# Scatter windows of 144 destination columns in place of 160 in a four-layer graph network

## Chip, cores and metric

One Trainium2 chip, one of its cores. The metric is the device time of one execution in microseconds (us), lower is better. Before: 2755.7 us, the median of three runs (2754.37 to 2758.44).

## The reference, cut to what matters

6250 nodes with 128 features each, 100000 edges sorted by destination node, four message-passing layers. Layers 0 and 1 (the first two) add relu(x[src] + edge attribute) into the destination node, then an MLP with a batch norm; layers 2 and 3 (the last two) add x[src] alone and apply another MLP.

```python
...
dst = jnp.minimum((6250 * jax.random.uniform(..., (100000,)) ** 2.0).astype(jnp.int32), 49999)
_o = jnp.argsort(dst, stable=True)
src = src[_o]
dst = dst[_o]
...
msg = jax.nn.relu(x[src] + edge_attr)
agg = jax.ops.segment_sum(msg, dst, num_segments=N_NODES)
h = (x + agg) @ W1l + b1l
...
agg = jax.ops.segment_sum(x[src], dst, num_segments=x.shape[0])
h = (1.0 + eps) * x + agg
...
```

## The kernel before, in words

The edges are cut into 196 groups of 512 (`SUPERS`), and four groups make a turn of 2048 edges, 49 turns to a layer (`TURNS`). A turn has two windows (`HALVES`), each of two groups, 1024 edges. Since the edges are sorted, the destinations of one window lie close together; the window begins at the smallest of them and is `WIN` columns wide. How many such windows, laid side by side, are needed for the widest pair of groups is worked out on the chip (`reached_f`, line 1352: the multiples of `WIN` that do not exceed the widest pair's spread are counted into `rounds`), and every scatter loop runs `rounds` times.

One edge stage (layers 0 and 1, `edges`) has five steps for each turn:

- POOL gathers the source rows from the node table in HBM with indirect DMAs, 128 rows of 512 bytes each (line 675), 16 to a turn; in two turns of each layer one group's four are replaced by row loads on SP's queue. Its buffer `xg` holds three turns, and POOL waits on `summed` (line 672) before it uses one again.
- ACT copies the edge attributes into PSUM (line 759), DVE adds the gathered rows to them (`slot_sum`, line 1131), ACT applies the relu to half a turn (line 786).
- DVE builds a one-hot matrix (`set_windows`, line 1077): for each of 16 columns of 128 edges, `WIN` columns of which the one of the edge's destination is 1. So it writes 16 x `WIN` elements to a partition.
- PE multiplies messages by one-hots (`edge_windows`, line 1510): 16 float32 matmuls to a turn, `WIN` columns each, into `psG`. The trace shows two matmul records for each.
- DVE adds the two windows to the accumulator `acc` at columns read from `first_i` (`add_windows`, line 1061, the instruction in line 1030).

Beside that, while the edge stages run, DVE and PE count how often each source meets each destination for the first 34 turns of edges (lines 1096, 1117 and 1494), ACT evicts the counts (line 742), and SP stores them to HBM (line 587). In the final turn of a layer the order on DVE is another one: the one-hot of the final turn is built ahead of its message sums (line 1153), and the windows of the last two turns are added at the end.

Layers 2 and 3 (`counted_edges`) use those counts: PE multiplies features by counts (line 1537, 147 matmuls of 456 columns for a group of 12 units), which stands for the first 34 turns; the last 15 turns are still gathered and scattered as windows. So PE alternates half a group of counts (72 or 75 matmuls) with one turn's windows (`late_windows`, line 1552, again 16 float32 matmuls of `WIN` columns and 32 records). POOL gathers those turns with 16 indirect DMAs each (line 695), 240 to a layer, into two buffers: turn k+2 waits until PE has finished the windows of turn k (`reduced`, line 691), and on the indices that ACT copies when a turn's rows have landed (line 831). DVE builds the one-hots (line 1202) and adds the windows. SP loads the next half group of counts, some 2.8 MB, when PE has finished with the buffer (line 596). In the last layer DVE adds a bias over all nodes in one instruction (line 1228), behind its first one-hots.

The turns of the counted layers are numbered 0 to 14 below, and POOL's gathers in one such layer 1 to 240.

What the change touches: the constant `WIN` (line 33), and by it lines 36, 313, 315, 320 (sizes), 651 (the offsets of the windows), 1061, 1077, 1187, 1202, 1510 and 1552.

```python
first_i[:, q, :] = min(pair_f + round_off, NODES)
...
rows[p, c, w] = (loc_all[p, c] - round_off == iota[w])
...
acc[:, first:first + WIN] += psG[:, q, h * WIN:(h + 1) * WIN]
...
```

Of the kernel before, what the change touches and what calls it, by code (L numbers as in the profile page):

```python
# [29 lines left out]
HALVES = (range(0, 2), range(2, SLOTS))  # L30
WINDOWS = len(HALVES)
PAIRED = SUPERS // 2
WIN = 160
BLOCKS = -(-NODES // P)
PADDED = BLOCKS * P
ACC = PADDED + WIN
GB = 4
# [151 lines left out]

assert TURNS % 2 == 1 and 2 * SLOTS * EPP * WIN <= CELL_RING * CB  # L190
assert SUPERS % SLOTS == 0 and OVERLAP % EPP == 0 and SECOND <= P
# [27 lines left out]
def gnn_kernel(nc, x, src, dst, edge_attr, W1, b1, gamma, beta, W2, b2,  # L219
               w1a, b1a, w1b, b1b, eps1, w2a, b2a, w2b, b2b, eps2, out):  # L220
    with ExitStack() as ctx:
        ctx.enter_context(nc.allow_non_contiguous_dma(reason="columns of biases"))

        def sb(name, shape, dt=F32):
            return ctx.enter_context(nc.sbuf_tensor(name, shape, dt))

        def sem(name):
# [84 lines left out]

        hot = hid[:, 0:2 * SLOTS * EPP * WIN].rearrange("p (q u j w) -> p q u j w", q=2, u=SLOTS, j=EPP)

        late_hot = rows_h[:, :, :].rearrange("p b d -> p (b d)")[:, 0:2 * SLOTS * EPP * WIN].rearrange(
            "p (q c w) -> p q c w", q=2, w=WIN)


        cell_room = sb("cell_room", [P, max(UPG * HALF_B * CW, CELL_RING * CB)], F16)
        last_hot = cell_room[:, 0:2 * SLOTS * EPP * WIN].bitcast(F32).rearrange("p (u j w) -> p u j w", u=SLOTS, j=EPP)  # L320
        cells = cell_room[:, 0:CELL_RING * CB].rearrange("p (r c) -> p r c", c=CB)
# [1393 lines left out]
```

## Time and profile before

| What | us |
|---|---|
| median of the three runs | 2755.7 |
| the profiled execution's own time | 2753.93 |
| its span, first to last instruction | 2752.1 |
| POOL busy | 1941.4 (71% of the span) |
| PE busy | 1908.3 (69%) |
| DVE busy | 1701.1 (62%) |
| ACT busy | 735.4 (27%) |

The edge stages of layers 0 and 1 lie between about 60 and 990 us and between 1030 and 2005 us; the counted edges of layers 2 and 3 between 2066 and 2377 us and between 2409 and 2726 us. A busy share is an average over these stages; which engine sets the pace has to be read in each of them. Busy times do not hold the gaps between two instructions of one engine, which the trace calls "issue" where the engine waits for nothing that the profile shows.

### The profile page before, as it was taken

To read this page: it belongs to the slowest core of one execution; us is meant where nothing else is said; L and a number is where in the kernel's file an instruction comes from. 1 tells how busy PE (TensorE), PEld (TensorE's weight loads), DVE (VectorE), ACT (ScalarE), POOL (GpSimd) and SP (SyncE) were. 2 spreads that over 40 slices of the span, in tenths; PEclk is the share of its full clock that TensorE was granted. 3 is DMA by queue.
4 is the path that set the end of the run, shared out by engine and by line. 5 is a ranking of instruction groups with operands and counts; after the bars stand their busy time and mean duration, and the time that the engine had idled before them with its cause. 6 is when DMAs were issued, how large, how long until landed. Compare 5 with 4: busy or idle time off the path is not lost.

```text
span 2752.1 us, 35065 instructions
## 1 busy us (share of the span) xinstructions
PE 1908.3 (69%) x9399; PEld 1278.4 (46%) x9399; DVE 1701.1 (62%) x2880; ACT 735.4 (27%) x1002; POOL 1941.4 (71%) x2048
## 2 busy tenths in 40 slices
PE   2476656566656672666566666656578999989999
PEld 2354444344444442435444444434444566546555
DVE  7797677777777764777777777777774221342212
ACT  4132222222222251333333333333361000210001
POOL 6777777777777727777777777777707777377773
PEclk8687777787888786878878888888878999999999
DMA  6343433343434333444444444444426566465653
GB/s 199 97 144 107 129 107 122 113 128 114 135 114 136 120 112 98 132 138 127 149 128 149 135 156 141 156 149 149 146 92 203 190 219 198 135 208 186 211 193 101
DMA packets 228544, 396.82 MB, mean 144 GB/s; under 512 B 43080, under 2 KB 133020, under 8 KB 228388
## 3 DMA queue, kind: packets, MB, share of 16 engines
q0 software_dynamic: 65024, 133.30, 18.1%
q1 hardware_dynamic: 111684, 162.15, 17.2%
q10 hardware_dynamic: 51680, 99.63, 10.4%
q8 instruction: 57, 0.93, 0.1%
q14 instruction: 99, 0.81, 0.1%
HBM read 333.10 MB, written 61.81 MB: 143 GB/s over the span
## 4 chain that ended last, share of the span: by engine, by line
POOL 52%; PE 22%; issue 18%; DVE 4%; DMA 3%; ACT 1%; DVEq 1%; POOLq 0%; SPq 0%; ACTq 0%
POOL xg L675 50%; PE psA L1537 14%; PE psG L1552 4%; POOL xg L695 2%; DMA xg<-node_table,src_all 2%; PE psG L1601 2%; PE psA L1609 1%; DVE xp_room L1131 0%; DVE hid L1077 0%; PE psG L1631 0%; DVE acc L1030 0%; DVE hid L1247 0%; PE psA L1618 0%; DVE xp_room L955 0%; DVEq L1052 0%
## 5 line engine op out<-in xcount | busy, mean ns | idle before, releaser
L675 POOL DMA_INDIRECT xg<-node_table,src_all x1520 | 1437.3, 946 | 506.9 <-issue 458.3
L1510 PE MATMUL psG<-hid,xp_room 128*128 128x160 f32 x3072 | 614.2, 376 | 421.6 <-DVE hid L1077 411.7
L1510 PEld LDWEIGHTS psG<-hid,xp_room 128*128 128x128 f32 x3072 | 595.3, 255 | 466.3 <-issue 455.8
L1494 PE MATMUL psA<-cell_room,xp_room 128*128 128x512 f16 (+1 forms) x2336 | 551.6, 388 | 299.2 <-ACT count_out L742 253.3
L1117 DVE TENSOR_SCALAR cell_room<-psG,cell_all 128x932 f16<-128x932 int16 x1088 | 684.6, 688 | 0.0
L695 POOL DMA_INDIRECT xg<-node_table,idx x480 | 468.1, 975 | 250.6 <-issue 248.7
L759 ACT COPY psG<-xp_room 128x512 f32<-128x512 f32 x384 | 226.5, 590 | 1257.7 <-DVE xp_room L1131 1226.5
L1494 PEld LDWEIGHTS psA<-cell_room,xp_room 128*128 128x128 f16 x2336 | 230.7, 103 | 582.7 <-ACT count_out L742 287.8
L1131 DVE TENSOR_TENSOR xp_room<-psG,xg 128x512 f32<-128x512 f32 x380 | 257.3, 677 | 385.8 <-DMA xg<-node_table,src_all 372.2
L1030 DVE TENSOR_TENSOR acc<-acc,row_slot 128x38 f32 x192 | 38.7, 202 | 385.3 <-ACT row_slot L838 360.7
L1077 DVE SCALAR_TENSOR_TENSOR hid<-loc_all,round_off,psG 128x2560 f32<-128x2560 f32 x96 | 274.7, 2862 | 0.1
L1537 PE MATMUL psA<-cell_room,xp_room 128*128 128x456 f16 x1200 | 241.7, 361 | 21.8 <-DVE xp_room L1253 21.8
L1537 PE MATMUL psA<-hid,xp_room 128*128 128x456 f16 x1152 | 234.8, 364 | 0.0
L786 ACT ACTIVATE xp_room<-xp_room 128x1024 f32<-128x1024 f32 x196 | 206.0, 1052 | 7.6 <-DVE xp_room L1023 4.5
L1030 DVE TENSOR_TENSOR acc<-acc,psG 128x160 f32 x272 | 87.3, 321 | 193.2 <-issue 148.3
L1537 PEld LDWEIGHTS psA<-cell_room,xp_room 128*128 128x128 bf16 x1200 | 115.7, 97 | 142.8 <-issue 26.6
L742 ACT CAST count_out<-psA 128x1862 f16<-128x1862 f32 x96 | 163.3, 1701 | 57.1 <-PE psA L1494 57.0
L1537 PEld LDWEIGHTS psA<-hid,xp_room 128*128 128x128 bf16 x1152 | 111.8, 97 | 118.4
L1552 PE MATMUL psG<-rows_h,xg 128*128 128x160 f32 x960 | 136.3, 299 | 6.2 <-DMA xg<-node_table,idx 6.2
L1552 PEld LDWEIGHTS psG<-rows_h,xg 128*128 128x128 f32 x960 | 133.6, 190 | 10.3 <-DMA xg<-node_table,idx 7.2
L838 ACT COPY row_slot<-psA 128x456 f32<-128x456 f32 x16 | 8.6, 538 | 360.2 <-PE psA L1537 360.2
L1096 DVE TENSOR_TENSOR xp_room<-psG,src_lo_all 128x768 f16<-128x768 int16 (+2 forms) x132 | 93.2, 727 | 0.0
(156 smaller groups left out, 804.5 us busy)
## 6 DMA issues: line engine op xcount, KB each, us to landing
xp_room<-in_edge_attr_dram ACTq DMA_DIRECT2D x95, 768.0 KB
cell_room<-count_store SPq DMA_DIRECT2D x16, 2850.0 KB
count_store<-count_out SPq DMA_DIRECT2D x96, 465.5 KB
hid<-count_store SPq DMA_DIRECT2D x16, 2736.0 KB
xg<-node_table,src_all POOLq DMA_INDIRECT x1520
xp_room<-in_edge_attr_dram ACTq DMA_DIRECT2D x95, 256.0 KB
row_slot<-node_table SPq DMA_DIRECT2D x1024, 0.5 KB
hid<-node_table SPq DMA_DIRECT2D x1024, 0.5 KB
```

The costliest lines, as they stand in the source:

```text
L675: nc.gpsimd.indirect_dma_start(xg[:, n % XG, u, j, :], None, x if n < RAW_TURNS else table, bass.IndirectOffsetOnAxis(ap=src_all[:, s, j:j ...
L695: nc.gpsimd.indirect_dma_start(xg[:, q, u, j, :], None, table, bass.IndirectOffsetOnAxis(ap=idx[:, q, u, j:j + 1], axis=0),).then_inc(row_ ...
L742: act.copy(count_out[:, k % 2, :], psA[:, :, :].rearrange("p k c -> p (k c)")[:, 0:CB]).then_inc(count_evicted, 1)
L759: act.copy(ea_stage, ea[:, n % RING, u, :, :].rearrange("p j d -> p (j d)")).then_inc(ea_staged, 1)
L786: act.activation(half, half, ACT.Relu).then_inc(msg_ready, 1)
L1077: nc.vector.scalar_tensor_tensor(out=rows.rearrange("p u j w -> p (u j) w"), in0=loc.unsqueeze(2).broadcast_to((P, SLOTS * EPP, WIN)), sca ...
L1117: nc.vector.tensor_scalar(cells[:, c % CELL_RING, c0:c1], iota_bank[:, 0:c1 - c0], float(c0), cell_all[:, c:c + 1], ALU.add, ALU.is_equal) ...
L1131: nc.vector.tensor_tensor(ea[:, n % RING, u, :, :].rearrange("p j d -> p (j d)"), ea_stage, rows, ALU.add).then_inc(summed, 1)
L1494: last = nc.tensor.matmul(psA[:, bank, 0:w], src_hot[:, hots(n) % 2, at, :], cells[:, c % CELL_RING, c0:c0 + w], start=first, stop=end)
L1510: last = nc.tensor.matmul(psG[:, q, h * WIN:(h + 1) * WIN], ea[:, t, u, j, :], rows[:, u, j, :], start=(u == slots[0] and j == 0), stop=(u ...
L1537: last = nc.tensor.matmul(out_cols, xp[:, b, part, :], counts[h][:, :, i * CW:(i + 1) * CW], start=(b == 0 and part == 0), stop=(b == BLOC ...
L1552: last = nc.tensor.matmul(psG[:, q, h * WIN:(h + 1) * WIN], xg[:, q, u, j, :], late_hot[:, q, u * EPP + j, :], start=(u == slots[0] and j ...
```

## The change

One constant is smaller: the windows have 144 columns. The one-hots, the scatter matmuls, the window adds and the window offsets follow from it; no instruction is added, removed or moved.

```diff
--- before.py
+++ after.py
@@ -30,7 +30,7 @@
 HALVES = (range(0, 2), range(2, SLOTS))
 WINDOWS = len(HALVES)
 PAIRED = SUPERS // 2
-WIN = 160
+WIN = 144
 BLOCKS = -(-NODES // P)
 PADDED = BLOCKS * P
 ACC = PADDED + WIN
```

## Rows read from the trace of the kernel before

**Rows 1.** The page's chain that ended last, shares of the span by engine.

```profile
POOL 52%; PE 22%; issue 18%; DVE 4%; DMA 3%; ACT 1%; DVEq 1%; POOLq 0%; SPq 0%; ACTq 0%
```

**Rows 2.** Groups by line and shape: busy us, mean ns, then idle before and releaser.

```profile
L1510 PE MATMUL psG<-hid,xp_room 128*128 128x160 f32 x3072 | 614.2, 376 | 421.6 <-DVE hid L1077 411.7 <-DVE acc L1030 9.7 <-issue 0.2
...
L1077 DVE SCALAR_TENSOR_TENSOR hid<-loc_all,round_off,psG 128x2560 f32<-128x2560 f32 x96 | 274.7, 2862 | 0.1
...
L1030 DVE TENSOR_TENSOR acc<-acc,psG 128x160 f32 x272 | 87.3, 321 | 193.2 <-issue 148.3 <-PE psG L1552 22.3 <-PE psG L1510 3.8
...
L1096 DVE TENSOR_TENSOR xp_room<-psG,src_lo_all 128x768 f16<-128x768 int16 x84 | 78.8, 938 | 0.0
...
L1096 DVE TENSOR_TENSOR xp_room<-psG,src_lo_all 128x128 f16<-128x128 int16 x40 | 10.4, 269 | 0.0
```

**Rows 3.** POOL's groups by line from 100 to 988 us.

```profile
L675 POOL DMA_INDIRECT xg<-node_table,src_all x712 | 671.9, 944 | 217.1 <-issue 214.7 <-DVE xp_room L1131 2.4
```

**Rows 4.** DVE's waits from 100 to 988 us: us in total, times, longest.

```profile
DVE xp_room L1131 <- DMA xg<-node_table,src_all: 157.4, 73, 5.2
```

**Rows 5.** Timeline at layer 0's end: start us, us, instruction, idle before and releaser.

```profile
987.16 0.95 POOL L675 DMA_INDIRECT xg<-node_table,src_all  x1 [0.31 <-issue]
...
989.95 0.69 DVE L1131 TENSOR_TENSOR xp_room<-psG,xg 128x512 f32<-128x512 f32 x1 [1.30 <-ACT psG L759]
```

**Rows 6.** The same at the end of layer 1's edges.

```profile
1999.41 0.94 POOL L675 DMA_INDIRECT xg<-node_table,src_all  x1 [0.30 <-issue]
...
2001.97 0.69 DVE L1131 TENSOR_TENSOR xp_room<-psG,xg 128x512 f32<-128x512 f32 x1 [2.37 <-DMA xg<-node_table,src_all]
```

**Rows 7.** Chain pieces on PE in layers 2 and 3: start us, us, what.

```profile
2105.58 4.35 PE psG L1552 x32
...
2728.51 0.89 PE psA L1618 x8
```

**Rows 8.** Timeline of layer 2's counted edges.

```profile
2110.95 0.94 POOL L695 DMA_INDIRECT xg<-node_table,idx  x1 [0.87 <-issue]
...
2349.42 0.94 POOL L695 DMA_INDIRECT xg<-node_table,idx  x1 [0.30 <-issue]
...
2352.13 0.20 ACT L831 COPY idx<-src_all 128x16 int32 x1 [17.98 <-DMA xg<-node_table,idx]
2352.23 0.38 SPq L596 DMA_DIRECT2D cell_room<-count_store  x1
...
2369.40 0.94 POOL L695 DMA_INDIRECT xg<-node_table,idx  x1 [0.30 <-issue]
2370.90 4.51 PE L1552 MATMUL psG<-rows_h,xg 128*128 128x160 f32 x32
```

**Rows 9.** Timeline of layer 3's counted edges.

```profile
2415.98 16.59 PE L1537 MATMUL psA<-cell_room,xp_room 128*128 128x456 f16 x75 [11.49 <-DVE xp_room L1253]
...
2428.14 6.67 DVE L1228 TENSOR_TENSOR rows_x<-rows_x,bias_last 128x6272 f32<-128x6272 f32 x1
2428.17 7.46 POOL L695 DMA_INDIRECT xg<-node_table,idx  x1 [0.30 <-issue]
...
2678.17 0.95 POOL L695 DMA_INDIRECT xg<-node_table,idx  x1 [0.30 <-issue]
...
2683.85 2.44 PE L1552 MATMUL psG<-rows_h,xg 128*128 128x160 f32 x16 [3.47 <-DMA xg<-node_table,idx]
2684.12 0.20 ACT L831 COPY idx<-src_all 128x16 int32 x1 [5.15 <-DMA xg<-node_table,idx]
...
2686.13 14.88 PE L1537 MATMUL psA<-cell_room,xp_room 128*128 128x456 f16 x75
...
2718.11 0.94 POOL L695 DMA_INDIRECT xg<-node_table,idx  x1 [0.30 <-issue]
2719.71 4.51 PE L1552 MATMUL psG<-rows_h,xg 128*128 128x160 f32 x32
```

**Rows 10.** A stretch: PE, PEld, DVE, ACT, POOL busy (count), PE clock, DMA share, GB/s.

```profile
2364.00:2370.00 6.00, 6.00 (x31) 2.91 (x30) 0.00 (x0) 0.00 (x0) 4.48 (x6) 1.00 0.21 53
```

## The prediction

> **What bounds the kernel now.** I read the chain that ended last first. POOL holds 52% of it, PE 22%, and 18% is issue [rows 1]; nearly all of that issue stands between two gathers. The change shortens work on DVE and PE only, so the question is where either of them sets the end.
>
> In the edge stages neither does. From 100 to 988 us POOL runs 712 gathers, 671.9 us busy and 217.1 us between them, 889.0 us in a stretch of 888 us [rows 3]: one gather every 1.249 us, without a hole. Its wait on DVE's sums is 2.4 us in all, no longer apiece than the usual issue gap. DVE waits for gathers instead, 157.4 us in 73 waits [rows 4]. So POOL's own rate is the time of a turn, about 16 x 1.249 = 19.98 us.
>
> In layers 2 and 3 the chain goes along PE, and the change looks as if it would pay there: the windows of a turn take 4.35 us of it [rows 7]. But next to it POOL goes on at one gather per 1.249 us. PE's turn is half a group of counts and the windows, 18.95 us (14 steps from the windows at 2105.58 to those at 2370.90 [rows 7, 8]); POOL's is 19.98. POOL starts ahead, PE catches up by 1 us a turn, and both arrive together: layer 2's gather 240 is issued at 2369.40 and PE begins that turn's windows at 2370.90; in layer 3 the pair is 2718.11 and 2719.71 [rows 8, 9]. In layer 3 PE already waits for rows, 3.47 us at 2683.85 [rows 9]. What PE saves there is mostly handed to a longer wait for gathers.
>
> **The pieces.** A float32 scatter record takes 4.35 / 32 = 136 ns at 160 columns, and one of 128 columns 0.89 / 8 = 111 ns [rows 7]. Halfway, 144 columns cost 124 ns, so 32 records save 0.40 us (0.43 if the whole time went with the columns). The one-hot falls from 2560 to 2304 elements: from 128 to 768 elements another DVE operation rises by 669 ns, 1.045 ns an element [rows 2], so 256 elements are 0.27 us of 2.86; 0.29 if proportional. A window add of 321 ns loses at most a tenth, 0.03 us [rows 2]; I take 0.015 each. No queue gets or loses an instruction: SP, ACT and POOL issue what they issued.
>
> **Edge stages, the turns.** 98 turns x (0.27 + 2 x 0.015) is 29 us of DVE and 98 x 0.40 is 39 us of PE, and I cost both at nothing. The cover is POOL's unbroken stream. If it were gone (DVE as the bound) the 29 us would count; that is a rival below. PE waits there for the one-hot, 411.7 us in all [rows 2], and has room besides.
>
> **Edge stages, the ends.** In layer 1 the last gather is issued at 1999.41 and DVE's sum starts 2.56 us later, released by that DMA [rows 6]. Everything before it is hidden; behind it lie one half turn of scatter (16 records, 0.20 us less) and two adds (0.03): 0.23 us. In layer 0 the last sum starts at 989.95, 2.79 us after its gather, released by ACT [rows 5], since DVE's one-hots had pushed the sums back. Two one-hots and adds before it give 0.6 us, but the rows land no sooner than 987.16 + 2.56 = 989.72, so 0.23 us of it counts, and the same 0.23 behind it: 0.46 us. Bounds 0.2 (nothing of the push back) and 0.85 (the landing was earlier than in layer 1).
>
> **Layer 2.** Gather 33 waits 0.87 us in place of 0.30 [rows 8]: it needs PE's windows of turn 0 to be done, which now happens 0.40 us earlier, so POOL's later gathers move from 2369.40 to 2369.00. With no count load in the way a turn's rows land 2.71 us after the last issue (2349.42 to 2352.13) [rows 8]; so PE's second half of turn 14 can start at 2371.71, where it started at 2370.90 + 2.18 = 2373.08: 1.37 us sooner at best. The other bound comes from turn 13. PE, now ahead, ends each half group earlier, and so SP's count load starts earlier against the last gathers of that turn. With such a load in front, rows landed 5.95 us after the issue (2678.17 to 2684.12) [rows 9]. If that hits turn 13 (issue 2349.02), PE's next second half comes one shortened turn, 18.95 - 0.40 = 18.55 us, after 2354.97, at 2373.52: 0.44 us later than now. Nothing tells which, so I take the middle, 0.47, and add the shorter half and adds, 0.23: 0.70 us (-0.2 to 1.6).
>
> **Layer 3.** No wait for PE there, but the long bias add holds POOL: DVE starts it at 2428.14, and the gather of 2428.17 takes 7.46 us, ending 0.82 us after DVE does [rows 9]. The one-hot and adds in front are 0.30 us shorter, so DVE starts and ends 0.30 us earlier, and with it POOL: gather 240 at 2717.81. This start falls within 0.02 us of the end of the gather before. By the row I take the 0.30; if that gather is caught as well, its rest and a full gather follow and POOL is 0.17 us late instead. The Trainium skill (SBUF — State Buffer, section "Who interferes with whom") says that whoever issues first holds the shared ports and the other blocks fully; by it the earlier gather would finish and DVE would wait those 0.02 us, and layer 3 would keep 0.28 us. No run here shows it yet. Landing at 2.71 allows PE's last second half at 2720.52, against 2719.71 + 2.18 = 2721.89; with turn 12 landing 5.95 us after its issue again (2683.82) PE's own two turns of 18.55 us end at 2720.92. The gain is between 0.97 and 1.37; I take 1.17, and 0.23 for the rest: 1.40 us (0.65, with the 0.30 turned into 0.17 the other way, to 1.6).
>
> **Sum.** 0.46 + 0.23 + 0.70 + 1.40 = 2.8 us. The profiled execution goes from 2753.93 to 2751.1; the median of the runs lies 1.8 above it, so the runs should show 2755.7 - 2.8 = 2752.9 us. Bounds added, the gain is 0.9 to 4.3 us. All of that is below 0.2% (5.5 us), about what a measurement of this kernel can tell from no change.
>
> **Rivals.** *PE keeps its gain in the counted layers.* 30 turns x 0.40 = 12 us, plus the 0.7 of the edge ends: 2743. It needs POOL to have slack; its issue times leave none at the end of either layer [rows 8, 9]. 6%.
>
> *DVE was the true bound of the edge stages*, POOL only following through its buffers: 29 us less, 2727. POOL would show waits on `summed`; it shows 2.4 us [rows 3]. 2%.
>
> *Slower: the count loads fall on the last gathers.* In both counted layers the last turn lands at 5.95 in place of 2.7 us: layer 2's second half at 2374.95 (+1.87), layer 3's at 2723.76 (+1.87), less 2 x 0.23 and the 0.69 of layers 0 and 1: 2.6 us slower, 2758.3. It decides only if a load still runs when gather 240 is issued. Against it: the load that was issued at 2352.23 [rows 8] is through by 2364, since from there to 2370 the DMA engines are 21% busy [rows 10], and layer 3 has no load after turn 12. 9%.
>
> *Slower by the clock.* After an idle stretch of 11.49 us PE's first 75 count matmuls take 16.59 us, where they otherwise take 14.88: 1.7 us for starting on the lower of the two clocks [rows 9]. PE will now wait some 1.4 us in each late turn, several us in some. The wait of 3.47 us at 2683.85 was followed by 14.88 us at full rate [rows 9], so no fall is seen at that length. If the last three waits of both layers each cost 1.7 us, POOL's schedule hides all but the last one, so 3.4 us for the two layers against the 2.8: 2756.3. The Trainium skill (TensorE: Matmul & The Clock Gate, section "HAM oscillation — how this bites in real kernels") warns of just such waits between bursts; the row disagrees up to 3.47 us. 4%.
>
> *The change does not do what it says*: a pair of groups spread over 144 columns or more would set `rounds` to 2, and each turn would build one-hots, multiply and add twice. In layers 2 and 3 PE alone would have 30 x 3.95 = 118 us more, less some 16 us of waits: about 2855. From the reference's inputs I work out the widest pair: 129 columns, so `rounds` stays 1. 1%.
>
> **How the numbers follow.** The forecast has 78%, 2752.9 us. Its bounds (2751.4 to 2754.8), widened by how far runs lie from their median (1.3 below, 2.7 above), give about 2750 to 2757.5. The two slower rivals reach to 2758.3; the faster ones lie far out and are left out. The range that holds 8 in 10 is 2749.5 to 2757.5. Faster by over 0.2%: the two faster rivals and a sliver of the forecast, 10%. Slower by over 0.2%: the doubled rounds and the upper tail of the two slower rivals, 4%. Within 0.2%: 86%.
>
> **What would show it.** In the changed profile POOL should still issue a gather each 1.249 us in the edge stages, with 712 in the same stretch; the one-hot should take 2.59 us, 32 late scatter records 3.95 us. DVE's wait for gathers in layer 0 should grow from 157 towards 170 us, since the saved time turns into waiting. In layers 2 and 3 PE's waits for rows should rise by some 10 us in all (30 x 0.40 less what is gained), with the last gather issued 0.4 and 0.3 us earlier after the layer's start. A gather rate other than 1.249 us, or gather starts that move with PE's, would make the prediction wrong.

## Result and profile after

The change is slower: 2758.47 us against 2754.12 us, medians of 22 runs each, ratio 1.0015 (95% interval 1.0009 to 1.0021), some 4 us. One of the 22 runs of the kernel before took 6318 us; without it the median is 2754.09. Forecast were 2752.9 us and a range up to 2757.5. The profiled execution after has 2755.56 us and a span of 2753.7 us, near the lower end of its runs (2755.15 to 2761.76).

The prices of the pieces came out as worked out. The groups by line and shape of the changed kernel (busy us, mean ns, then idle before and releaser), against [rows 2]:

```profile
L1510 PE MATMUL psG<-hid,xp_room 128*128 128x144 f32 x3072 | 549.5, 354 | 302.0 <-DVE hid L1077 291.1 <-DVE acc L1030 10.1 <-issue 0.4
L1077 DVE SCALAR_TENSOR_TENSOR hid<-loc_all,round_off,psG 128x2304 f32<-128x2304 f32 x96 | 249.2, 2595 | 0.0
L1552 PE MATMUL psG<-rows_h,xg 128*128 128x144 f32 x960 | 127.8, 292 | 11.6 <-DMA xg<-node_table,idx 11.6
L1030 DVE TENSOR_TENSOR acc<-acc,psG 128x144 f32 x272 | 82.6, 304 | 190.6 <-issue 142.8 <-PE psG L1552 23.7 <-PE psG L1510 5.1
```

The one-hot takes 2.595 us (2.862 before), the add 304 ns (321). POOL's group and DVE's wait from 100 to 988 us stand beside [rows 3, 4], and the chain by engine beside [rows 1]:

```profile
L675 POOL DMA_INDIRECT xg<-node_table,src_all x712 | 672.1, 944 | 217.1 <-issue 213.1 <-DVE xp_room L1131 4.0
```

```profile
DVE xp_room L1131 <- DMA xg<-node_table,src_all: 176.1, 76, 5.4
```

```profile
POOL 52%; issue 18%; PE 17%; DMA 6%; DVE 5%; DVEq 1%; ACT 1%; POOLq 0%; ACTq 0%; SPq 0%
```

The gather stream of the edge stages did not move: 712 gathers, 217.1 us between them, to the tenth what it was. DVE waits for gathers 176.1 us in place of 157.4. In the chain PE gave 5 points away and DMA took 3: landings are waited for that were not on the path before. So the 4 us lie where the stream is not: between the last gather of a layer and the first of the next, called a **hand-over** below. The timeline of layer 2, first more of the kernel before, beside [rows 8], then the changed kernel:

```profile
2329.43 0.94 POOL L695 DMA_INDIRECT xg<-node_table,idx  x1 [0.30 <-issue]
...
2332.98 4.51 PE L1552 MATMUL psG<-rows_h,xg 128*128 128x160 f32 x32
...
2333.31 0.37 SPq L596 DMA_DIRECT2D hid<-count_store  x1
...
2377.10 3.03 PE L1601 MATMUL psG<-acc,w_first 128*128 128x512 f32 x6 [1.68 <-DVE acc L1030]
```

```profile
2329.49 2.12 PE L1552 MATMUL psG<-rows_h,xg 128*128 128x144 f32 x16
2329.82 0.37 SPq L596 DMA_DIRECT2D hid<-count_store  x1
...
2330.04 0.94 POOL L695 DMA_INDIRECT xg<-node_table,idx  x1 [0.30 <-issue]
...
2335.39 3.83 PE L1552 MATMUL psG<-rows_h,xg 128*128 128x144 f32 x16 [3.78 <-DMA xg<-node_table,idx]
...
2370.01 0.94 POOL L695 DMA_INDIRECT xg<-node_table,idx  x1 [0.30 <-issue]
2372.21 4.08 PE L1552 MATMUL psG<-rows_h,xg 128*128 128x144 f32 x32
...
2377.57 0.74 DVE L1030 TENSOR_TENSOR acc<-acc,psG 128x144 f32 x2
...
2378.37 4.25 PE L1601 MATMUL psG<-acc,w_first 128*128 128x512 f32 x6 [2.07 <-DVE acc L1030]
```

The first gather line is turn 12's last one in both. Before, PE began turn 12's windows 3.55 us behind it; now PE begins them 0.55 us ahead of it, and SP issued the next 2.7 MB of counts at 2329.82, 0.22 us ahead of that gather. Those rows were used at 2335.39, 5.35 us after their gather's issue instead of some 2.7. Then 16 records took 3.83 us in place of 2.1 to 2.2: the granted clock is 0.57 in this stretch, so TensorE ran mostly at the lower of its two levels, 1.2 GHz. Two turns later PE is still behind: it begins the last windows 2.20 us after the last gather (1.50 before), and 6 products of the MLP take 4.25 us (granted clock 0.65), 3.03 before. From the last gather to layer 3's first one it is 41.60 us, 39.44 before.

### The profile page after: what moved, and what is told of

The parts are those of the page before. It is cut to its first block, busy times and chain, and to the rows that moved or that the text cites. A ratio compares the mean times of both kernels' runs of the same rounds, so it can differ in the third digit from the quotient of the medians.

```text
span 2753.7 us, 35065 instructions
## 1 busy us (share of the span) xinstructions
PE 1890.0 (69%) x9399; PEld 1215.4 (44%) x9399; DVE 1662.3 (60%) x2880; ACT 736.5 (27%) x1002; POOL 1941.5 (71%) x2048
## 4 chain that ended last, share of the span: by engine, by line
POOL 52%; issue 18%; PE 17%; DMA 6%; DVE 5%; DVEq 1%; ACT 1%; POOLq 0%; ACTq 0%; SPq 0%
POOL xg L675 46%; PE psA L1537 10%; POOL xg L695 6%; DMA xg<-node_table,src_all 5%; PE psG L1552 2%; PE psG L1601 2%; PE psA L1609 1%; DVE hid L1077 1%; DVE xp_room L1131 1%; DVEq L1052 1%; DVE acc L1030 0%; PE psG L1510 0%; DVE xp_room L1096 0%; PE psG L1631 0%; DVE hid L1247 0%
## 5 line engine op out<-in xcount | busy, mean ns | idle before, releaser
L1494 PE MATMUL psA<-cell_room,xp_room 128*128 128x512 f16 (+1 forms) x2336 | 603.3, 411 | 433.7 <-ACT count_out L742 295.7
L1510 PE MATMUL psG<-hid,xp_room 128*128 128x144 f32 x3072 | 549.5, 354 | 302.0 <-DVE hid L1077 291.1
L1510 PEld LDWEIGHTS psG<-hid,xp_room 128*128 128x128 f32 x3072 | 534.0, 252 | 348.9 <-issue 337.8
L1077 DVE SCALAR_TENSOR_TENSOR hid<-loc_all,round_off,psG 128x2304 f32<-128x2304 f32 x96 | 249.2, 2595 | 0.0
L1030 DVE TENSOR_TENSOR acc<-acc,psG 128x144 f32 x272 | 82.6, 304 | 190.6 <-issue 142.8
L1552 PE MATMUL psG<-rows_h,xg 128*128 128x144 f32 x960 | 127.8, 292 | 11.6 <-DMA xg<-node_table,idx 11.6
L1552 PEld LDWEIGHTS psG<-rows_h,xg 128*128 128x128 f32 x960 | 125.8, 195 | 15.6 <-DMA xg<-node_table,idx 12.5
```

Of the source, the lines that this page charges most:

```text
L1077: nc.vector.scalar_tensor_tensor(out=rows.rearrange("p u j w -> p (u j) w"), in0=loc.unsqueeze(2).broadcast_to((P, SLOTS * EPP, WIN)), sca ...
L1494: last = nc.tensor.matmul(psA[:, bank, 0:w], src_hot[:, hots(n) % 2, at, :], cells[:, c % CELL_RING, c0:c0 + w], start=first, stop=end)
L1510: last = nc.tensor.matmul(psG[:, q, h * WIN:(h + 1) * WIN], ea[:, t, u, j, :], rows[:, u, j, :], start=(u == slots[0] and j == 0), stop=(u ...
L1552: last = nc.tensor.matmul(psG[:, q, h * WIN:(h + 1) * WIN], xg[:, q, u, j, :], late_hot[:, q, u * EPP + j, :], start=(u == slots[0] and j ...
```

## Experiments

Three theories. **Clock**: PE, with less to do, waits more and runs at 1.2 GHz where its next work is on the path. **Loads**: a transfer that PE sets off now starts earlier and lands ahead of the last gathers of a turn. **DVE**: its earlier one-hots matter.

The table holds one trace of each kernel: hand-overs of layers 0, 1 and 2, from layer 3's last gather to the span's end, and two times counted from layer 0's last gather: when ScalarE issues a 1 MB load of edge attributes (lines 751 and 752, for a turn of the next layer), and when the last slot sum (line 1131) starts.

| kernel | layer 0 | layer 1 | layer 2 | layer 3 to end | load issue | last sum |
|---|---|---|---|---|---|---|
| before | 44.71 | 66.81 | 39.44 | 33.99 | 1.20 | 2.79 |
| e9 before | 46.36 | 67.28 | 39.42 | 32.69 | 0.84 | 3.37 |
| after | 44.52 | 67.55 | 41.60 | 32.98 | 1.16 | 2.74 |
| e5 after | 49.92 | 67.52 | 42.01 | 33.13 | -0.19 | 5.41 |
| e16 after | 47.69 | 66.96 | 41.85 | 33.45 | 0.46 | 4.47 |
| e1 144 early, 160 late | 44.38 | 65.86 | 38.90 | 32.79 | 0.98 | 2.57 |
| e2 160 early, 144 late | 45.60 | 66.33 | 42.22 | 33.27 | 2.10 | 3.69 |
| e3 one-hots 160 | 47.00 | 67.17 | 42.07 | 33.08 | 0.57 | 3.53 |
| e4, e15 counts held | 50.56, 50.78 | 65.90, 67.06 | 37.86, 37.94 | 32.14, 32.21 | 0.12, 0.33 | 5.07, 5.10 |
| e6 PE passes 160 | 46.16 | 66.94 | 39.01 | 32.30 | 2.58 | 4.17 |
| e7 busy PE | 47.75 | 67.79 | 40.42 | 36.01 | 1.25 | 2.84 |
| e8 busy, counts held | 48.20 | 68.04 | 38.85 | 33.11 | 1.70 | 3.29 |
| e14 attributes held | 45.27 | 67.50 | 41.82 | 33.52 | held | 2.65 |
| e10 both held | 46.59 | 67.51 | 37.89 | 32.18 | held | 2.57 |
| e13 both held, busy | 45.76 | 67.17 | 37.81 | 32.22 | held | 2.60 |
| e11 both held, 160 | 44.70 | 66.85 | 39.34 | 32.56 | held | 2.64 |
| e12 both held, PE 160 | 46.19 | 67.21 | 39.07 | 32.35 | held | 2.52 |

**Which layers (e1, e2).** Each constant use of `WIN` is split in two.

```diff
+WIN_E = 144   # layers 0 and 1; 160 in e2
+WIN_L = 160   # layers 2 and 3; 144 in e2
```

> 144 columns in layers 0 and 1 (one-hots, scatter matmuls, adds), 160 in layers 2 and 3. Clock theory (PE, with less to do, sits idle longer and finds the lower of its two clocks where its next matmuls are on the path): the end of layer 1's edges and the MLPs behind it lose 1.5 to 2 us, layers 2 and 3 run as before, so 1.0005 to 1.001 of before. Load theory (all of the loss comes from count loads that fall on the last gathers of layers 2 and 3): at or under 1.000. DVE theory (an earlier one-hot disturbs the edge stages' gathers): POOL's gather rate in layers 0 and 1 rises above 1.249 us.

Measured: 2756.07 us, ratio 0.9995 (0.9986 to 1.0004).

> 160 columns in layers 0 and 1, 144 in layers 2 and 3. Clock theory: waits for rows of over 3 us appear in layers 2 and 3, scatter records behind them take 239 ns in place of 122, and the first products of layer 2's MLP start slow; 1.0005 to 1.001 of before. Load theory: the same place, the whole loss of 1.0015, with landings of 5 to 6 us at the last turns and no slow records on the path. If the loss lay in the edge stages alone: 0.9995 to 1.000.

Measured: 2758.32 us, 0.9997 (0.9988 to 1.0006). The load theory had forecast the whole loss of 1.0015 for e2, which the time does not show. These two, e3 and e4 ran on a chip on which the kernel before itself stood at 2758.24 us; nothing was traced there that says why, so between chips only traces are compared here. Within that chip e1 is 2.3 us under e2, less than their runs spread. The clear sign is layer 2's hand-over: 38.90 with 160 late columns, 42.22 with 144.

**Which engine (e3, e6).** e3 builds one-hots of 160 columns, of which PE passes and DVE adds 144. e6 is its mirror: 144 built and added, 160 passed (in all but the last matmul of a turn; the 16 extra columns are a stretch of the next one-hot, and fall beside the window in PSUM).

```diff
# e3
-ea[:, t, u, j, :], rows[:, u, j, :],
+ea[:, t, u, j, :], rows[:, u, j, 0:PW],        # PW = 144, WIN = 160
# e6
-psG[:, q, h * WIN:(h + 1) * WIN], ea[:, t, u, j, :], rows[:, u, j, :],
+psG[:, q, h * PW:h * PW + w], ea[:, t, u, j, :], flat[:, at * WIN:at * WIN + w],   # PW = 160; w: PW, in the last WIN
```

> One-hots stay 160 wide on DVE, PE multiplies and DVE adds 144 columns. Clock theory and load theory (both start from a PE that is done sooner): 1.001 to 1.002 of before, as the whole change. DVE theory (the shorter one-hot does it): 1.000.

Measured: 2759.65 us, 1.0004 (0.9995 to 1.0013), under the 1.001 to 1.002 that was expected; layer 2's hand-over 42.07.

> One-hot build and window adds over 144 columns as in the change, but TensorE passes over 160 columns in all but the last record of each turn (the 16 extra ones lie beside the window in PSUM and are not added). VectorE does what it does in the change, TensorE what it did before. If the loss comes from TensorE being done earlier (its clock, or the count loads that it sets off): hand-over of layer 2 back to 39 to 40 us, ratio 0.999 to 1.000. If it comes from VectorE being done earlier: 41 to 42.5 us and 1.001 to 1.002 as in the change.

Measured: 2752.14 us, 0.9994 (0.9985 to 1.0003), 6.4 us under e5 on the same chip; hand-over 39.01. With DVE as in the change and PE as before the loss is gone; with PE as in the change and DVE's one-hots as before it is there. The DVE theory falls: the loss comes from PE being done earlier.

**The change and the kernel before again (e5, e9, e16).**

> The changed kernel once more, with a trace, beside the kernel before. Hand-over of layer 2 (last gather of layer 2 to first gather of layer 3): 39.4 us in the trace of before, 41.6 in that of the change. Clock and load theories: 41 to 42.5 us again, and a ratio of 1.001 to 1.002. If the loss were a matter of a single execution: hand-over 38.5 to 40, ratio 0.999 to 1.000. The last 16 scatter records of layers 0 and 1 take 2.2 us each if TensorE holds 2.4 GHz, 3.9 to 4.2 if it fell; the clock theory cannot say in which layer.

Measured: 2758.51 us, 1.0017 (1.0008 to 1.0026).

> The changed kernel on the same chip as the two single holds and their sum with a busy TensorE. Ratio 1.001 to 1.002 again; hand-over of layer 2 41.5 to 42.2 us; layer 0's end between 44.5 and 50 us, long where ScalarE issues the attribute load less than 0.6 us behind the last gather or ahead of it.

Measured: 2757.98 us, 1.0014 (1.0005 to 1.0023).

> The kernel before as it is, with a trace of its own. Ratio 0.999 to 1.001. It gives the hand-overs of a second execution at 160 columns: layer 2 to layer 3 should be 39 to 39.5 us again (39.44 in the first trace, 38.9 and 39.0 in the two other kernels whose late scatters pass 160 columns) by both theories; if it is 41 to 42, the loss there is not the change's. At layer 0's end the gap between the last gather's issue and ScalarE's attribute load (1.20 us in the first trace) says where this execution stands: above 1 us the last slot sum starts 1.59 us behind that load, below 0.6 us the load lands ahead of the gather.

Measured: 2754.36 us, 1.0001 (0.9992 to 1.001). Three traces of the change against two of the kernel before, means: layer 0 47.38 against 45.54 (+1.8), layer 1 67.34 against 67.05 (+0.3), layer 2 41.82 against 39.43 (+2.4), the end 33.19 against 33.34 (-0.15): +4.4 in all. The four gather streams are 0.8 us shorter, and the first begins 0.1 us later. That leaves 3.7, the difference of the mean spans, where the medians differ by some 4. Layer 2's part is in all three traces: a count load within 0.3 us of turn 12's last gather, and 16 records in 3.65 to 4.21 us behind it. In e5 the low clock lasted into the counts that follow (15.90 us in place of 14.88) and the MLP began at the full clock; in the other two the MLP began slowly. Layer 0's part varies, and e5 shows its cause. Its timeline:

```profile
986.34 0.39 ACTq L751 DMA_DIRECT2D xp_room<-in_edge_attr_dram  x1
...
986.53 0.95 POOL L675 DMA_INDIRECT xg<-node_table,src_all  x1 [0.30 <-issue]
986.76 0.50 ACTq L752 DMA_DIRECT2D xp_room<-in_edge_attr_dram  x1
...
991.94 0.69 DVE L1131 TENSOR_TENSOR xp_room<-psG,xg 128x512 f32<-128x512 f32 x1 [5.83 <-DMA xg<-node_table,src_all]
...
993.77 4.21 PE L1510 MATMUL psG<-cell_room,xp_room 128*128 128x144 f32 x16 [5.06 <-ACT xp_room L786]
```

ScalarE issues the attribute load when PE has scattered the turn before the last. Here that was 0.19 us ahead of the last gather, and the rows came when most of the load was through. Of the 5.4 us by which e5's hand-over exceeds that of the first trace of the change, 2.67 are the later sum, 1.98 the 16 records (4.21 us at a granted clock of 0.50, against 2.23) and 0.75 lie in the MLP. In the table a load 0.57 us or less behind the last gather (five traces, all with PE at 144) goes with a last sum at 3.53 to 5.41 us. From 0.84 us on it is 2.57 to 4.17, and the sum waits for ScalarE instead, whose attribute copy stands behind the load in its queue: sum start = load + 1.59 us in seven traces of eight. The eighth is e9 (0.84), whose sum still waits for its rows, to 3.37. With PE at 160 columns the load was issued 0.84 to 2.58 us behind the gather (before, e9, e2, e6), with PE at 144 and no hold in five traces of nine at 0.57 us or less.

**A busy PE (e7, e8).** Products of the identity matrix, in PSUM columns that nothing reads; e8 adds the hold on the count loads of e4.

```diff
+keep_busy(psA[:, 3, 512 - P:512], 10)     # last turn of layers 0, 1: ahead of its scatter
+keep_busy(psG[:, q, 512 - P:512], 6)      # ... and between its two halves
+keep_busy(psG[:, 3, 0:P], 10)             # layers 2, 3: ahead of the first product
```

> The change, and TensorE kept busy in the idle time ahead of the critical records: 10 matrix products of 128x128 ahead of the last turn's scatter of layers 0 and 1, 6 between its two halves, 10 between the last scatter of layers 2 and 3 and the first product of their MLP. Clock theory: the last 16 records of layers 0 and 1 take 2.2 us in both layers, the first 6 products of layer 2's MLP about 3.0 us in place of 4.25, hand-over of layer 2 about 40.3 us (1.2 less than in the change; the late landings stay), in sum 2 to 4 us less than the change. Load theory alone: hand-over 41.6 to 42.2, time as the change.

Measured: 2759.12 us, 1.0014 (1.0005 to 1.0023).

> The change with both remedies: count loads held until the rows of their turn have landed, and TensorE kept busy ahead of the critical records. If both theories hold: hand-over of layer 2 about 37 us (37.9 with the loads held alone), layer 1 about 65.9, layer 0 about 44.5, so 4 to 6 us less than the change, ratio 0.997 to 0.9985 to the kernel before. If only the loads count: as with the loads held alone, ratio 0.999.

Measured: 2757.18 us, 1.0012 (1.0003 to 1.0021). Both missed their times. The clock did as expected: 16 records in 2.13 us in layers 0 and 1 (granted clock 1.00), and layer 2's hand-over of 40.42 us in e7 (3.03 us for the first 6 products), 1.2 less than in the change. But the 10 products ahead of the last turn's scatter stood before work that was due: PE ran them at 988.01, and that scatter began at 990.25. In e7's layer 3 (36.01 us) a count load fell on the last gathers of turn 12 (a wait of 3.65 us for rows, 16 records in 4.21); in the three traces of the change this befell turn 11, which leaves PE a turn more to catch up. So these two do not tell what the clock costs at the ends of layers 0 and 1.

**Loads held (e4, e15, e14, and both in e10).** The count load waits until ScalarE has copied the indices, which it does when the turn's rows have landed (the first loads of a layer, with no rows under way, are not held). The attribute load of layer 0's last turn goes behind the last slot sum.

```diff
# e4 and e15, load_half on SP, cut
...
+if h:
     ...
+    sp.wait_ge(idx_ready[0], n)
+elif ...:
+    sp.wait_ge(idx_ready[1], landed)
 sp.dma_start(counts[h][:, :, :], ...)
# e14, edges on ACT
-if u == (SLOTS - 1 if n == RAW_TURNS else 1):
+if u == (SLOTS - 1 if n in (RAW_TURNS, TURNS - 1) else 1):
     load_behind(n - 1)
```

> The change, and SP holds each count load back until the rows of the turn whose windows PE is about to multiply have landed. Load theory: rows land 2.7 us after the last issue in each turn, PE's waits in layers 2 and 3 stay under 2 us, and the time falls to 0.999 of before. Clock theory: the long waits in layers 2 and 3 go with the late landings, so the slow records there go too, but the slow half turn at layer 1's end stays: 1.0000 to 1.0008.

Measured: 2754.77 us, 0.9991 (0.9982 to 1.0000), on the chip of e1 to e3.

> The change with the count loads held alone, on one chip with the attribute hold alone and the change as it is. Load theory: hand-over of layer 2 37.9 again, layer 0's end as it falls (2.6 to 5.4 us from last gather to last slot sum); median about 3.5 us under the change as it is, ratio 0.999 to 1.0. If the count loads have no part: the time of the change.

Measured: 2752.23 us, 0.9990 (0.9981 to 0.9999), 5.8 us under e16 on the same chip.

> The change with ScalarE's attribute load of layer 0's last turn held alone. Load theory: last gather of layer 0 to last slot sum 2.3 to 2.6 us, hand-over of layer 0 at most 46.6; layer 2's hand-over stays at 41.5 to 42.2. Median 0.9995 to 1.0005 of the kernel before, 1 to 3 us under the change as it is. If the attribute load has no part in the loss: the time of the change.

Measured: 2755.35 us, 1.0004 (0.9995 to 1.0013), 2.6 us under e16. Its eleven runs lie within 2.6 us (2754.55 to 2757.14), those of e15 within 7.4 (2749.53 to 2756.93): in the traces it is layer 0's end that varies, and with the hold the last sum starts at 2.65 us. Five of e16's eleven runs are at 2760 us or above, none of these.

> The change with both kinds of transfers held back: count loads of layers 2 and 3 until the rows of their turn have landed, and ScalarE's load of the next attributes in the last turn of layer 0 until the last slot sum has been made. Load theory: last gather of layer 0 to last slot sum 2.3 to 2.8 us in every execution (2.57 to 5.41 in the runs so far), hand-over of layer 0 44 to 44.8 us (46 to 46.5 if the last 16 records run at the low clock), of layer 2 about 37.9; the median 3 to 5 us under the change and under the kernel before, ratio 0.998 to 0.999. Clock theory alone: still 1.000 to 1.0015, with the last 16 records of layers 0 or 1 at 3.8 to 4.2 us.

Measured: 2750.49 us, 0.9985 (0.9976 to 0.9995), runs from 2749.61 to 2752.27. **This beats both kernels**: the kernel before is at 2753.64 us on this chip, and e13, which has the same holds, is 7.0 us under e16 on its chip. The attribute hold did not remove the low clock at layer 0's end, where the last 16 records take 3.73 us. Its timeline at layer 2's end, in two stretches:

```profile
2330.11 2.12 PE L1560 MATMUL psG<-rows_h,xg 128*128 128x144 f32 x16
...
2330.95 0.94 POOL L703 DMA_INDIRECT xg<-node_table,idx  x1 [0.30 <-issue]
...
2333.55 2.23 PE L1560 MATMUL psG<-rows_h,xg 128*128 128x144 f32 x16 [1.31 <-DMA xg<-node_table,idx]
...
2334.20 0.37 SPq L604 DMA_DIRECT2D hid<-count_store  x1
...
2370.94 0.95 POOL L703 DMA_INDIRECT xg<-node_table,idx  x1 [0.30 <-issue]
...
2373.85 2.23 PE L1560 MATMUL psG<-rows_h,xg 128*128 128x144 f32 x16 [1.64 <-DMA xg<-node_table,idx]
...
2377.09 3.03 PE L1609 MATMUL psG<-acc,w_first 128*128 128x512 f32 x6 [1.02 <-DVE acc L1038]
```

The load now goes out after the rows are there, the last windows wait 1.64 us for rows alone, and the MLP starts at the full clock (3.03 us, granted clock 1.00).

**The two holds at other widths (e11, e12).**

> The same two holds on the kernel before, at 160 columns. Load theory: little to gain in layer 2 (its loads fall on gathers seldom: 39 us to 38.5), 0.3 to 1 us at layer 0's end; ratio 0.9985 to 1.0, and 0 to 2 us slower than the 144 columns with the holds. Clock theory: as fast as or faster than the 144 columns with the holds, since TensorE stays busier; last 16 records 2.4 us.

Measured: 2752.58 us, 0.9996 (0.9987 to 1.0005).

> 144 columns built and added, 160 passed by TensorE, with both holds. Clock theory: the fastest of the three with holds, ratio 0.998 to 0.999, last 16 records of layers 0 and 1 at 2.4 us in both. Load theory alone: between the other two, within 1 us of the 160 columns with the holds.

Measured: 2752.49 us, 0.9991 (0.9982 to 1.0000). With the loads out of the way the order turns round: 144 columns are 2.1 us faster than 160 (e10, e11), and PE passing 160 columns is worth nothing any more (e12). The intervals of e10 and e11 overlap a little; layer 2's hand-overs, 37.89 and 39.34, point the same way.

**What the low clock costs (e13).** e10 with 6 products between the halves of the last turn alone, in a wait of 2.0 to 2.2 us.

```diff
+if h and n % TURNS == TURNS - 1:
+    keep_busy(psG[:, q, 512 - P:512], 6)
```

> The change with both holds, and 6 products of 128x128 (12 records, 1.5 us at 2.4 GHz) on TensorE in the 2.0 to 2.2 us in which it waits between the two halves of the last turn of layers 0 and 1; nothing ahead of the first half this time. Clock theory: the last 16 records take 2.2 us in both layers (3.73 and 3.90 with the holds alone), hand-over of layer 0 about 45, of layer 1 about 66, so 2 to 3.5 us less than with the holds alone, ratio 0.997 to 0.998. If the low clock there costs nothing at the end, or does not hang on the wait ahead of it: the time of the holds alone, 0.9985.

Measured: 2751.02 us, 0.9986 (0.9977 to 0.9995): the time of the holds alone, though the last 16 records ran at the full clock (granted 1.00). PE's timeline at layer 1's end, first e10, then e13:

```profile
2004.91 3.90 PE L1518 MATMUL psG<-cell_room,xp_room 128*128 128x144 f32 x16 [2.04 <-ACT xp_room L794]
2009.86 10.79 PE L1609 MATMUL psG<-acc,w_first 128*128 128x512 f32 x26 [1.05 <-DVE acc L1038]
2024.60 4.61 PE L1617 MATMUL psA<-hid,w_second 128*128 128x512 f32 x6 [3.95 <-ACT hid L907]
```

```profile
2003.62 1.50 PE L1508 MATMUL psG<-ident 128*128 128x128 f32 x12
2004.96 2.20 PE L1524 MATMUL psG<-cell_room,xp_room 128*128 128x144 f32 x16
2008.21 10.79 PE L1615 MATMUL psG<-acc,w_first 128*128 128x512 f32 x26 [1.05 <-DVE acc L1038]
2022.95 5.63 PE L1623 MATMUL psA<-hid,w_second 128*128 128x512 f32 x6 [3.95 <-ACT hid L907]
```

Of the 1.7 us saved on the scatter 1.0 is lost 15 us later, where 6 products take 5.63 us (granted clock 0.50) in place of 4.61 (0.63); the whole hand-over is 67.17 against 67.51 us. In layer 0 it is 45.76 against 46.59. So at the ends of layers 0 and 1 the low clock is worth about 1 us in the traces and nothing that the times show; in layer 2 it comes behind a late landing, and the holds remove it.

## Why the prediction failed, step by step

**Edge stages, the turns**: right. POOL's stream hides 29 us of DVE and 39 us of PE, and neither shows. Of the signs named, the gather rate and DVE's wait (176 us) came true; PE's waits for rows in layers 2 and 3 rose from 6.2 to 11.6 us, about half of the 10 forecast.

**Prices**: right. 2.595 us for the one-hot (2.59), and 32 late records in 4.08 us as the timeline gives them (4.51 before): 0.43 less, the upper of the two values considered.

**Layer 0's end (0.46 us gained): the step that failed first.** The landing of the last gather was taken as a fixed 2.56 us. [rows 5] said that the last sum was released by ScalarE, which was put down to late one-hots; it was the attribute load, 1.59 us ahead of it in ScalarE's queue, which the working did not contain. When PE ends earlier that load can move in front of the last gather. Measured +1.8 us in the mean of three traces against two, and up to 5.2 (e5 against before).

**Layer 1's end (0.23)**: +0.3 us. The 16 records at the low clock cost 1.5 us there in two of the three traces of the change, and the MLP gave most of it back.

**Layer 2 (0.70, bounds -0.2 to 1.6): the mechanism was named and mis-sized; in the means this is the larger part, +2.4 us.** A count load against the last gathers was the lower bound, set on turn 13 and priced at 0.44 us. It struck turn 12. The working had let PE meet the stream where it met it before, near turn 14; but 12 turns of its own 0.40 us are 4.8, more than the 3.55 us by which PE was behind turn 12's last gather before. Behind the late landing came what the bound left out: 16 records largely at 1.2 GHz, and a low clock at the MLP's start, 33.24 us from the first product to layer 3's first gather in two of the three traces, 31.74 before. From layer 2's first gather to layer 3's: 342.62 us before, 344.46 after, a loss of 1.8. With the loads held it is 340.82 at 144 and 342.62 at 160 columns: a gain of 1.8, above the 1.6 of the upper bound.

**Layer 3 (1.40)**: not resolved. From its first gather to the end it takes 343.26 and 341.96 us in two traces of the kernel before and 342.09, 342.12 and 342.42 in three of the change; with holds 341.17 (e10) against 341.96 (e11), 0.8 gained. The piece of it that was told apart came true. These lines of the changed kernel's timeline answer to [rows 9]:

```profile
2429.70 0.95 POOL L695 DMA_INDIRECT xg<-node_table,idx  x1 [0.30 <-issue]
2430.62 6.68 DVE L1228 TENSOR_TENSOR rows_x<-rows_x,bias_last 128x6272 f32<-128x6272 f32 x1
2430.95 7.17 POOL L695 DMA_INDIRECT xg<-node_table,idx  x1 [0.30 <-issue]
```

The long gather is 7.17 us, 0.29 less than 7.46, and the one before it, 0.03 us of which lie behind DVE's start, was not caught: it took 0.95 us. The rule of the Trainium skill that the prediction weighed (SBUF — State Buffer, section "Who interferes with whom") agrees as far as the gathers go; the 0.02 us it would cost DVE are below what the rows show.

**The rivals.** *Count loads on the last gathers* had the right kind of cause and, at 2758.3 us, almost the measured time, but by accident: it set the load on the last turn of both counted layers. The argument against it, that no load runs when gather 240 is issued, held and did not matter, since a late turn 12 is enough. *The clock* was dismissed because a wait of 3.47 us was followed by a full-rate stretch [rows 9]; one row cannot exclude it. In the change 2.07 us of waiting came before 4.25 us for 6 products, and in e5 2.08 us before 3.03 us, so the length of the wait does not decide alone. The Trainium skill's warning about waits between bursts (TensorE: Matmul & The Clock Gate, section "HAM oscillation — how this bites in real kernels") holds here in kind, though in layer 1 most of the price at the scatter came back in the MLP. Both rivals were weighed as alternatives, 9% and 4%. In layer 2 they are one chain: the late landing makes the wait. Together with layer 0's attribute load they took the forecast gain of 2.8 us and some 4 us more.

Still open: what puts PE's end before or behind the last gather in a given execution, what layer 3 gained, and why the kernel before stood 4 us higher on the chip of e1 to e4.

## What to carry over

Before costing a faster engine at nothing, list every transfer that is issued when it finishes, carry the saving forward turn by turn, and set each issue time against the gathers that the next engine waits for: here a load issued up to 0.2 us ahead of a layer's last gather or 0.6 us behind it made the last sum up to 2.8 us later. A gain of some 2 us in such a kernel shows only once those loads wait until what is urgent has landed. The holds add no instruction to PE, DVE, ACT or POOL (e10's profile counts as many of each as before), and they also narrow the runs (2.7 us wide in e10, 6.9 in e5).

## What was not expected of the hardware

A small gather that is issued at about the same time as a large load begins late. The DMA view of e5 from 988 to 990 and from 990 to 992 us (q10 is ScalarE's load, q0 the gathers; packets, MB, share of 16 engines); the gather was issued at 986.53:

```profile
DMA packets 296, 0.61 MB, mean 303 GB/s; under 512 B 0, under 2 KB 0, under 8 KB 296
...
q10 hardware_dynamic: 296, 0.61, 87.3%
```

```profile
DMA packets 252, 0.45 MB, mean 225 GB/s; under 512 B 48, under 2 KB 48, under 8 KB 252
...
q10 hardware_dynamic: 220, 0.39, 50.3%
q0 software_dynamic: 32, 0.07, 8.4%
```

For 2 us 296 packets of the load ran and none of a gather; the last gather's 32 packets came behind 510 of the load's 544. The Trainium skill (DMA: Bandwidth & Descriptors, section "Queues, rings and completion order") has each DMA engine go round the queues that have work, a packet at a time; by that a gather that is ready is served between the load's packets. In the changed kernel from 2334 to 2336 us that is what the view shows (q1 is SP's count load of 2.7 MB, which is still running):

```profile
q1 hardware_dynamic: 376, 0.69, 88.1%
q0 software_dynamic: 64, 0.13, 16.8%
```

These are turn 12's last gather and the next one, between the load's packets. But the first of them has its first packet 4.05 us after its issue; at the same place before, and in e10, it is 1.65 us. At layer 0's end it is 1.65 us before and 4.32 in e5. So these records do not contradict the rule. They show a gather whose first packet comes late, by 2.4 and 2.7 us here; where that time goes is not shown.
